# Other warm-ups for TensorE, weights rounded in halves, and EPS added on GpSimd: a conditional MLP with LayerNorm on one core

## The chip, the cores and the metric

The kernel runs on one core of a Trainium2 chip, in one launch. The metric is the device time in microseconds (us) of that core, as the median of the timed runs. The engines are TensorE (PE, its weight loads PEld), VectorE (DVE), ScalarE (ACT), GpSimd (POOL) and SyncE (SP), which issues most DMAs.

## The reference

For each of 16 batches `x[b]` is 512x512. A condition per batch, read at run time, chooses a network; then follow a residual and a LayerNorm over the last axis:

```python
out_nr  = gelu(x @ w1_nr + b1_nr) @ w2_nr + b2_nr          # condition 0
out_tsr = gelu(x @ w1_tsr + b1_tsr) @ w2_tsr + b2_tsr      # condition 1
h = gelu(x @ w1_sr + b1_sr)                                # condition 2, w1_sr is 512x1024
out_sr = gelu(h @ w2_sr + b2_sr) @ w3_sr + b3_sr           # w2_sr is 1024x512
y = x + chosen
return (y - mean(y)) * rsqrt(var(y) + EPS) * gamma + beta
```

All is float32. The conditions of the sixteen batches are 0, 2, 0, 0, 0, 0, 0, 1, 2, 2, 1, 2, 0, 2, 2, 1: seven of kind 0 (`NR`), three of kind 1 (`TSR`), six of kind 2 (`SR`).

## The kernel before

**Precision.** Each fp32 operand is split into a part rounded to fp32r (`hi`) and the rest (`lo`), and each product of 128x128 by 128x512 is three matmuls: hi·hi, hi·lo and lo·hi (`product`, L243). A batch of kind 0 or 1 has 2 x 16 products, 96 matmuls; one of kind 2 has 32 + 32 + 16 products, 240 matmuls.

**Who does what.** SyncE loads the transposed x (`stage`), the rows of x (`y`) and the weights (`w_raw`, two chunks of 128x512 to a pair). For each batch ScalarE makes `x_hi`, the GELU as `g_hi`, and the GELU again unrounded in the PSUM bank; VectorE takes the differences `x_lo` and `g_lo`. TensorE's last layer leaves four tiles (t = 0 to 3, 128 rows each) in banks 4 to 7. GpSimd has added the bias to the rows of x (`add_bias`, L616); VectorE adds these to the bank (`residual`, L482), takes the statistics (`stats`, `moments`), adds EPS to the variances of two tiles at once (`variance`, L499, semaphore `s_var`), and subtracts the mean and multiplies by gamma (`centre`, L494). GpSimd raises variance + EPS to -0.5 (`deviations`, L620), ScalarE multiplies by that (L437), GpSimd adds beta (`shift`, L628), and SyncE stores. Each engine runs its own program in order; semaphores join them. ScalarE frees a bank for the next batch (`s_acc`) when it takes the centred tile. In the last batch the tiles go one by one (`body_end`).

**Weights.** The first w chunks of kind 0 are made by VectorE and ScalarE at the start. Those of the other kinds are split on GpSimd, in pairs (`split_hi` L590, `split_lo` L595), between its other work in the first batches.

**The start.** TensorE first runs warm-ups on a tile of ones: nine matmuls of 128x512 and fourteen of 128x128 in bf16 (L373, L375), whose result is unused. Then it reads the first condition and starts batch 0 (kind 0). The contraction has four chunks c = 0 to 3. For c = 0 and 1 the order is: four matmuls of x_hi and w_hi (which = 0, output columns j = 0 to 3), four with x_lo (which = 1), four with w_lo (which = 2). They wait for `s_first` (x_hi, from ScalarE, L444), `s_first_w` (w_hi, from VectorE, L570), `s_nr` and `s_x01` (the lo parts, L560). VectorE's order there is: cast of w chunk 0, x_lo, w_lo of chunk 0, then the same of chunk 1, then the lo parts of chunks 2 and 3.

Of the kernel before, what the change touches and what calls it, by code (L numbers as in the profile page):

```python
# [5 lines left out]
P = 128  # L6
NBATCH = 16
T = 512
H = 512
HC = H // P  # L10
TT = T // P
EPS = 1e-5
# [25 lines left out]
FINISHED_BY_OTHERS_END = TT - 1  # L38


N_WARM, N_WARM_SHORT = 9, 14


def conditional_mlp(nc, x, x_t, cond, weights, bias_cols, rows, out):
# [3 lines left out]
    with ctx:  # L48
# [3 lines left out]
        def sem(name):  # L52
            return ctx.enter_context(nc.semaphore(name))
# [50 lines left out]
        s_y, s_acc = sem("s_y"), sem("s_acc")  # L104
        s_row = [sem(f"s_x_row{t}") for t in range(TT)]
        s_xb, s_ev, s_bn, s_mv = sem("s_xb"), sem("s_ev"), sem("s_bn"), sem("s_mv")
        s_var = sem("s_var")
        s_own = sem("s_own")
        s_rstd, s_rstd_end = sem("s_rstd"), sem("s_rstd_end")
        s_v, s_v_end = sem("s_v"), sem("s_v_end")  # L110
# [4 lines left out]
        def take(eng, s, n=1):  # L115
            eng.wait_ge(s, n)
            eng.sem_inc(s, -n)  # L117
# [124 lines left out]
        def _(eng):  # L242
# [36 lines left out]
            def part(j, c, which):  # L279

                dst, n, w = bank[j][:, :], bass.ts(j, P), W1[NR] + c
                a, b = (w_lo if which == 2 else w_hi), (x_lo if which == 1 else x_hi)
                return eng.matmul(dst, a[:, w, n], b[:, c, :], start=c == 0 and which == 0, stop=c == HC - 1 and which == 2)

            def step(kind, read_next):
                if kind == NR:
                    take(eng, s_x01, 1)
                    for c in range(2):
                        eng.wait_ge(s_first, c + 1)
                        eng.wait_ge(s_first_w, c + 1)  # L290
                        for which in range(3):
                            if which == 1:
                                if c == 0:
                                    eng.wait_ge(s_nr, 1)
                                else:
                                    take(eng, s_x01, 1)
                                    x_taken(0)
                            if which == 2:
                                eng.wait_ge(s_nr, 2 + c)
                            for j in range(HC):  # L300
                                part(j, c, which)
                        if c == 0:
                            read_next()
                    take(eng, s_x23, 1)
                    for c in (2, 3):
                        if c == 3:
                            take(eng, s_x23, 1)
                            x_taken(1)
                        eng.wait_ge(s_first, 3 + c)
                        if c == 2:  # L310
                            eng.wait_ge(s_nr, 4)
                        for j in range(2):
                            part(j, c, 0)
                            part(j, c, 1)
                        eng.wait_ge(s_nr, 3 + c)
                        for j in range(2):
                            sums = part(j, c, 2)
                            if c == 3:
                                sums.then_inc(s_h, 1)
                    for j in (2, 3):  # L320
                        for c in (2, 3):
                            for which in range(3):
                                sums = part(j, c, which)
                        sums.then_inc(s_h, 1)
                    eng.wait_ge(s_nr, 8)
                    last_layer(W2[kind], ORDER, claim=True)
                    return
# [42 lines left out]
                last_layer(W3[SR], ORDER_SR, claim=False)  # L370

            for _ in range(N_WARM):
                eng.matmul(bank[7][:, :], ones[:, 0:P], ones, start=True, stop=True)  # L373
            for _ in range(N_WARM_SHORT):
                eng.matmul(bank[7][:, 0:P], ones[:, 0:P], ones[:, 0:P], start=True, stop=True)  # L375
            eng.sem_inc(s_acc, 4)
# [87 lines left out]
        def _(eng):  # L464
# [32 lines left out]
            def variance(t, n=1):  # L497
                take(eng, s_mv, n)
                eng.tensor_scalar(var_eps[:, t:t + n], mv[:, t:t + n, 1], EPS, None, ALU.add).then_inc(s_var, n)  # L499
# [15 lines left out]
            def body(kind, read_next):  # L515
                read_next()
                hidden(kind)
                split_x(0, s_x01, 2)
                split_x(1, s_x23, 2)
                eng.wait_ge(s_rows, 16)  # L520
                for t in range(0, TT, 2):
                    residual(kind, t)
                    residual(kind, t + 1)
                    stats(kind, t)
                    stats(kind, t + 1)
                    moments(kind, t)
                    moments(kind, t + 1)
                    variance(t, 2)
                    centre(kind, t)
                    centre(kind, t + 1)  # L530

# [35 lines left out]

            for c in range(2):
                eng.wait_ge(s_w_piece[c], 16)
                eng.tensor_copy(w_hi[:, c, :], w_raw[:, c, :]).then_inc(s_first_w, 1)  # L570
                x_low(c, c + 1, (s_nr, s_x01)[c])
                eng.wait_ge(s_first_w, c + 1)
                w_low(c, 0)
            x_low(2, 3, s_nr)
            x_low(3, 4, s_x23)
# [10 lines left out]
        def _(eng):  # L586
# [29 lines left out]
                        eng.tensor_tensor(y[:, t, :], y[:, t, :], row[:, kind, :], ALU.add).then_inc(s_xb, 1)  # L616

            def deviations(t, n):
                take(eng, s_var, n)
                eng.tensor_tensor(rstd[:, t:t + n], var_eps[:, t:t + n], power[:, t:t + n], ALU.pow).then_inc(s_rstd, n)  # L620

            def deviation_end(t, done=s_rstd):
# [149 lines left out]
```

## Time and profile before the change

| | us |
|---|---|
| median of 3 timed runs | 559.62 (559.47 to 559.8) |
| the profiled execution | 559.41 |
| its span | 557.7 |
| PE busy | 549.6 (99%) |
| DVE busy | 273.9 (49%) |
| POOL busy | 248.3 (45%) |
| ACT busy | 213.5 (38%) |

The span reaches from the first to the last instruction that the profiler saw in one execution. A row of a timeline gives an instruction's start and duration, or of several of one form in a row (x4) the time from the first one's start to the last one's end. The ends of matmuls are modelled and overlap with the next one's start, so the pace is read from the starts. A row of weight loads (PEld) stands for the matmul that follows it.

### The profile page before, as it was taken

Reading aid. Unit: us, or ns where it says so; the run is one execution under the profiler, and the core shown is the slowest. Engines: PE = TensorE matmul, PEld = TensorE weight load, DVE = VectorE, ACT = ScalarE, POOL = GpSimd, SP = SyncE. Lnnn points to the kernel's source line nnn. Section 1 sums busy time; section 2 is a strip of 40 time slices with the busy share of each in tenths; the row PEclk is TensorE's granted clock in tenths of the full one; section 3 lists DMA queues with packets and bytes.
Section 4 is the critical chain, followed back from the end, with each engine's and each line's share of the span. In section 5 each row is a group of like instructions: output and inputs, shape, how many; then the busy total and the mean of one; then the engine's idle time right before and its main releaser. Section 6 shows DMA issues by size and latency. Waiting matters only on the chain. (4 is left out here: it accounts for less than half of the span.)

```text
span 557.7 us, 8222 instructions
## 1 busy us (share of the span) xinstructions
PE 549.6 (99%) x2423; PEld 453.4 (81%) x2424; DVE 273.9 (49%) x448; ACT 213.5 (38%) x328; POOL 248.3 (45%) x196
## 2 busy tenths in 40 slices
PE   9999999999999999999999999999999999999994
PEld 6888888888888888888888888888888888888883
DVE  5660176775856956114710569112765105601657
ACT  5451336145244354214421452424255124513351
POOL 0979898765674575300430046600174300430056
PEclk9999999999999999999999999999999999999998
DMA  8876405245344444200320044400244100410032
GB/s 313 339 237 190 152 7 196 100 151 188 109 155 145 156 150 141 84 0 0 138 87 0 1 158 142 150 0 0 75 150 159 66 0 29 154 43 0 0 135 91
DMA packets 26370, 61.28 MB, mean 110 GB/s; under 512 B 3058, under 2 KB 3314, under 8 KB 26226
## 3 DMA queue, kind: packets, MB, share of 16 engines
q1 hardware_dynamic: 26208, 60.97, 31.9%
q8 instruction: 6, 0.10, 0.1%
q10 hardware_dynamic: 146, 0.13, 0.1%
q14 instruction: 10, 0.08, 0.1%
HBM read 44.31 MB, written 16.78 MB: 110 GB/s over the span
## 5 line engine op out<-in xcount | busy, mean ns | idle before, releaser
L467 DVE TENSOR_TENSOR g_lo<-bank,g_hi 128x512 fp32r<-128x512 f32 x112 | 77.5, 692 | 251.0 <-DVEq L117 250.9
L415 ACT ACTIVATE g_hi<-bank,bcol 128x512 fp32r<-128x512 f32 x112 | 77.9, 695 | 165.9 <-ACTq L117 164.7
L620 POOL TENSOR_TENSOR rstd<-var_eps,power 128x2 f32<-128x2 f32 x30 | 21.0, 699 | 239.7 <-POOLq L117 239.7
L616 POOL TENSOR_TENSOR y<-y,row 128x512 f32<-128x512 f32 x64 | 95.7, 1514 | 49.1 <-POOLq L117 48.9
L437 ACT ACTIVATE y<-y,rstd 128x512 f32<-128x512 f32 x63 | 42.3, 717 | 166.3 <-ACTq L117 166.3
L244 PE MATMUL bank<-w_hi,g_hi 128*128 128x512 f32 x256 | 99.6, 389 | 0.0
L245 PE MATMUL bank<-w_lo,g_hi 128*128 128x512 f32 x256 | 99.6, 389 | 0.0
L246 PE MATMUL bank<-w_hi,g_lo 128*128 128x512 f32 x256 | 99.6, 389 | 0.0
L244 PE MATMUL bank<-x_hi,w_hi 128*128 128x512 f32 x240 | 93.4, 389 | 0.0
L245 PE MATMUL bank<-x_lo,w_hi 128*128 128x512 f32 x240 | 93.4, 389 | 0.0
L246 PE MATMUL bank<-x_hi,w_lo 128*128 128x512 f32 x240 | 93.4, 389 | 0.0
L628 POOL TENSOR_TENSOR y<-y,row 128x512 f32<-128x512 f32 x63 | 79.5, 1296 | 0.0
L244 PE MATMUL bank<-g_hi,w_hi 128*128 128x512 f32 x192 | 74.7, 389 | 0.0
L245 PE MATMUL bank<-g_lo,w_hi 128*128 128x512 f32 x192 | 74.7, 389 | 0.0
L246 PE MATMUL bank<-g_hi,w_lo 128*128 128x512 f32 x192 | 74.7, 389 | 0.0
L416 ACT ACTIVATE bank<-bank,bcol 128x512 f32<-128x512 f32 x112 | 74.3, 664 | 0.0
L244 PEld LDWEIGHTS bank<-w_hi,g_hi 128*128 128x128 f32 x256 | 48.1, 188 | 10.0
L245 PEld LDWEIGHTS bank<-w_lo,g_hi 128*128 128x128 f32 x256 | 48.1, 188 | 10.0
L246 PEld LDWEIGHTS bank<-w_hi,g_lo 128*128 128x128 f32 x256 | 48.1, 188 | 9.9
L472 DVE TENSOR_TENSOR x_lo<-stage,x_hi 128x1024 fp32r<-128x1024 f32 x30 | 51.6, 1757 | 4.3 <-DVEq L117 4.3
L245 PEld LDWEIGHTS bank<-x_lo,w_hi 128*128 128x128 f32 x240 | 45.1, 188 | 9.3
L246 PEld LDWEIGHTS bank<-x_hi,w_lo 128*128 128x128 f32 x240 | 45.1, 188 | 9.3
(42 smaller groups left out, 580.2 us busy)
## 6 DMA issues: line engine op xcount, KB each, us to landing
y<-x SPq DMA_DIRECT2D x64, 256.0 KB, 3.6
out<-y SPq DMA_DIRECT2D x63, 256.0 KB, 2.5
stage<-x_t SPq DMA_DIRECT2D x31, 512.0 KB, 3.3
w_raw<-weights SPq DMA_DIRECT2D x17, 512.0 KB, 5.1
row<-rows SPq DMA_DIRECT2D x1, 1280.0 KB, 11.0
stage<-x_t SPq DMA_DIRECT2D x2, 256.0 KB, 3.2
w_raw<-weights SPq DMA_DIRECT2D x2, 256.0 KB, 4.0
out<-y SPq DMA_DIRECT2D x1, 128.0 KB, 1.9
```

Of the source, the lines that this page charges most:

```text
L244: eng.matmul(dst, a_hi, b_hi, start=first, stop=False)
L245: eng.matmul(dst, a_hi, b_lo, start=False, stop=False)
L246: return eng.matmul(dst, a_lo, b_hi, start=False, stop=final)
L415: eng.activation(g_hi[:, slot, :], psum, ACT.Gelu, bias=b)
L416: eng.activation(psum, psum, ACT.Gelu, bias=b).then_inc(s_g, 1)
L437: eng.activation(y[:, t, :], y[:, t, :], ACT.Copy, scale=rstd[:, t:t + 1]).then_inc(s_n, 1)
L467: eng.tensor_tensor(g_lo[:, slot, :], psum, g_hi32[:, slot, :], ALU.subtract).then_inc(s_gs, 1)
L472: eng.tensor_tensor(x_lo[:, c, :], stage[:, f, :, :], x_hi32[:, c, :], ALU.subtract).then_inc(done, n)
L616: eng.tensor_tensor(y[:, t, :], y[:, t, :], row[:, kind, :], ALU.add).then_inc(s_xb, 1)
L620: eng.tensor_tensor(rstd[:, t:t + n], var_eps[:, t:t + n], power[:, t:t + n], ALU.pow).then_inc(s_rstd, n)
L628: eng.tensor_tensor(y[:, t, :], y[:, t, :], row[:, R_BETA, :], ALU.add).then_inc(s_fin, 1)
```

## The change

Three edits.

1. TensorE's warm-ups are fifteen of 128x307 and seven of 128x128, where there were nine of 128x512 and fourteen of 128x128.
2. VectorE casts each of the first two w chunks in two halves of 256 columns. TensorE waits for a half before output columns j = 0 and j = 2 of the first pass, rather than for the whole chunk ahead of it.
3. For tiles 0 and 1 of the first fifteen batches, GpSimd adds EPS in `deviations`, ahead of its pow; VectorE hands it the moments (`s_moments`) and goes on to `centre`. For tiles 2 and 3 and for the last batch nothing changes.

```diff
-N_WARM, N_WARM_SHORT = 9, 14
+N_WARM, N_WARM_SHORT, WARM = 15, 7, 307
...
-                        eng.wait_ge(s_first_w, c + 1)
...
                             for j in range(HC):
+                                if which == 0 and j % 2 == 0:
+                                    eng.wait_ge(s_first_w, 2 * c + j // 2 + 1)
                                 part(j, c, which)
...
             for _ in range(N_WARM):
-                eng.matmul(bank[7][:, :], ones[:, 0:P], ones, start=True, stop=True)
+                eng.matmul(bank[7][:, 0:WARM], ones[:, 0:P], ones[:, 0:WARM], start=True, stop=True)
...
-                    variance(t, 2)
+                    if t == 0:
+                        take(eng, s_mv, 2)
+                        eng.sem_inc(s_moments, 2)
+                    else:
+                        variance(t, 2)
                     centre(kind, t)
...
                 eng.wait_ge(s_w_piece[c], 16)
-                eng.tensor_copy(w_hi[:, c, :], w_raw[:, c, :]).then_inc(s_first_w, 1)
+                for half in (slice(0, H // 2), slice(H // 2, H)):
+                    eng.tensor_copy(w_hi[:, c, half], w_raw[:, c, half]).then_inc(s_first_w, 1)
                 x_low(c, c + 1, (s_nr, s_x01)[c])
-                eng.wait_ge(s_first_w, c + 1)
+                eng.wait_ge(s_first_w, 2 * c + 2)
                 w_low(c, 0)
...
             def deviations(t, n):
-                take(eng, s_var, n)
+
+                if t == 0:
+                    take(eng, s_moments, n)
+                    eng.tensor_scalar(var_eps[:, t:t + n], mv[:, t:t + n, 1], EPS, None, ALU.add).then_inc(s_eps, n)
+                    take(eng, s_eps, n)
+                else:
+                    take(eng, s_var, n)
                 eng.tensor_tensor(rstd[:, t:t + n], var_eps[:, t:t + n], power[:, t:t + n], ALU.pow).then_inc(s_rstd, n)
```

TensorE at the start of the program, before (const-bfloat16-1.0 is the tile of ones):

```order
2 L373 MATMUL bank<-const-bfloat16-1.0 128x512 x9
3 L375 MATMUL bank<-const-bfloat16-1.0 128x128 x14
4 L136 TENSOR_LOAD cond_sb
5 L406 UNCONDITIONAL_BRANCH
6 L393 COMPARE_AND_BRANCH
```

and now:

```order
2 L374 MATMUL bank<-const-bfloat16-1.0 128x307 x15
3 L376 MATMUL bank<-const-bfloat16-1.0 128x128 x7
4 L136 TENSOR_LOAD cond_sb
5 L407 UNCONDITIONAL_BRANCH
6 L394 COMPARE_AND_BRANCH
```

The widths and counts of the warm-ups change and nothing else moves; the real matmuls behind them (L283) are in the same order.

VectorE at the end of batch 0, before (bn and mv are the statistics and moments):

```order
20 L487 BN_STATS bn<-bank 128x6 x2
21 L491 BN_AGGR mv<-bn 128x2 x2
22 L499 TENSOR_SCALAR var_eps<-mv 128x2
23 L494 SCALAR_TENSOR_TENSOR y<-bank,mv,row 128x512 x2
24 L482 TENSOR_TENSOR bank<-bank,y 128x512 x2
```

and now:

```order
20 L488 BN_STATS bn<-bank 128x6 x2
21 L492 BN_AGGR mv<-bn 128x2 x2
22 L495 SCALAR_TENSOR_TENSOR y<-bank,mv,row 128x512 x2
23 L483 TENSOR_TENSOR bank<-bank,y 128x512 x2
24 L488 BN_STATS bn<-bank 128x6 x2
```

The TENSOR_SCALAR on the variances of tiles 0 and 1 is gone, and the centring follows the moments.

GpSimd in the same place, before:

```order
18 L616 TENSOR_TENSOR y<-y,row 128x512 x2
19 L620 TENSOR_TENSOR rstd<-var_eps,power 128x2
20 L590 TENSOR_SCALAR w_hi<-w_raw 128x1024
21 L620 TENSOR_TENSOR rstd<-var_eps,power 128x2
22 L595 TENSOR_TENSOR w_lo<-w_raw,w_hi 128x1024
```

and now:

```order
18 L622 TENSOR_TENSOR y<-y,row 128x512 x2
19 L628 TENSOR_SCALAR var_eps<-mv 128x2
20 L632 TENSOR_TENSOR rstd<-var_eps,power 128x2
21 L596 TENSOR_SCALAR w_hi<-w_raw 128x1024
22 L632 TENSOR_TENSOR rstd<-var_eps,power 128x2
```

The addition stands between the last bias add and the first pow, ahead of the split of the weights.

## Rows read from the trace of the kernel before

**Rows 1.** The page: busy time, share of the span and instructions of each engine.

```profile
PE 549.6 (99%) x2423; PEld 453.4 (81%) x2424; DVE 273.9 (49%) x448; ACT 213.5 (38%) x328; POOL 248.3 (45%) x196
```

**Rows 2.** Stretches, TensorE alone: from:to, length, busy (instructions), granted clock, DMA share, GB/s.

```profile
6.00:550.00 544.00, 544.00 (x2402) 1.00 0.32 109
2.00:4.00 2.00, 2.00 (x6) 1.00 0.94 311
553.00:554.00 1.00, 0.00 (x0) 0.50 0.63 240
```

**Rows 3.** Timeline of the start, TensorE: start, duration, engine, line, what.

```profile
0.82 4.00 PE L373 MATMUL bank<-const-bfloat16-1.0 128*128 128x512 bf16 x9 [0.82 <-PEq L766]
2.05 0.15 PEld L373 LDWEIGHTS bank<-const-bfloat16-1.0 128*128 128x128 bf16 x1 [0.28 <-issue]
4.61 1.43 PEld L375 LDWEIGHTS bank<-const-bfloat16-1.0 128*128 128x128 bf16 x13 [0.28 <-issue]
6.07 0.55 PE L283 MATMUL bank<-x_hi,w_hi 128*128 128x512 f32 x1
6.46 0.63 PE L283 MATMUL bank<-x_hi,w_hi 128*128 128x512 f32 x2
6.69 0.62 PE L283 MATMUL bank<-x_hi,w_hi 128*128 128x512 f32 x2
7.15 1.07 PE L283 MATMUL bank<-x_lo,w_hi 128*128 128x512 f32 x4
8.96 1.07 PE L283 MATMUL bank<-x_hi,w_hi 128*128 128x512 f32 x4
11.68 0.39 PE L283 MATMUL bank<-x_hi,w_hi 128*128 128x512 f32 x1
```

**Rows 4.** Timeline of the end: TensorE's last matmul.

```profile
550.01 0.39 PE L246 MATMUL bank<-w_hi,g_lo 128*128 128x512 f32 x1
```

**Rows 5.** Timeline of the start, VectorE and ScalarE: where the first operands come from.

```profile
3.40 0.62 ACT L444 CAST x_hi<-stage 128x512 fp32r<-128x512 f32 x1 [0.57 <-DMA stage<-x_t]
4.43 0.43 DVE L570 CAST w_hi<-w_raw 128x512 fp32r<-128x512 f32 x1 [3.53 <-DMA w_raw<-weights]
7.05 0.43 DVE L570 CAST w_hi<-w_raw 128x512 fp32r<-128x512 f32 x1 [0.99 <-DMA w_raw<-weights]
7.40 0.68 DVE L560 TENSOR_TENSOR x_lo<-stage,x_hi 128x512 fp32r<-128x512 f32 x1
```

**Rows 6.** Timeline from batch 0 to batch 1, VectorE and GpSimd.

```profile
26.23 2.53 POOL L616 TENSOR_TENSOR y<-y,row 128x512 f32<-128x512 f32 x2
27.64 1.14 DVE L499 TENSOR_SCALAR var_eps<-mv 128x2 f32<-128x2 f32 x1
28.70 1.40 DVE L494 SCALAR_TENSOR_TENSOR y<-bank,mv,row 128x512 f32<-128x512 f32 x2
28.97 0.72 POOL L620 TENSOR_TENSOR rstd<-var_eps,power 128x2 f32<-128x2 f32 x1 [0.21 <-POOLq L117]
30.02 1.28 DVE L482 TENSOR_TENSOR bank<-bank,y 128x512 f32<-128x512 f32 x2
33.33 0.70 POOL L620 TENSOR_TENSOR rstd<-var_eps,power 128x2 f32<-128x2 f32 x1 [2.60 <-POOLq L117]
```

**Rows 7.** One line (durations ns min/median/max), and GpSimd's smallest operation.

```profile
L499 DVE TENSOR_SCALAR var_eps<-mv x34: 136/169/1142, 27.6 to 553.1; 128x2 f32<-128x2 f32 x30, 128x1 f32<-128x1 f32 x4
...
0.78 0.10 POOL L645 MEMSET power<- 128x4 f32 x1 [0.29 <-POOLq L766]
```

**Rows 8.** Timeline of batch 1: first g_lo and its matmul, fourth split and its matmul.

```profile
37.65 1.47 DVE L467 TENSOR_TENSOR g_lo<-bank,g_hi 128x512 fp32r<-128x512 f32 x2 [3.20 <-DVEq L117]
38.88 0.39 PE L244 MATMUL bank<-g_hi,w_hi 128*128 128x512 f32 x1
41.20 2.40 POOL L595 TENSOR_TENSOR w_lo<-w_raw,w_hi 128x1024 fp32r<-128x1024 f32 x1 [0.18 <-POOLq L117]
44.32 0.39 PE L244 MATMUL bank<-x_hi,w_hi 128*128 128x512 f32 x1
```

More of the change, by code:

```diff
@@ L106, in conditional_mlp @@
         s_xb, s_ev, s_bn, s_mv = sem("s_xb"), sem("s_ev"), sem("s_bn"), sem("s_mv")
-        s_var = sem("s_var")
+        s_moments, s_eps, s_var = sem("s_moments"), sem("s_eps"), sem("s_var")
         s_own = sem("s_own")
```

## The prediction

> **What bounds the kernel now.** I read the page's busy shares first: TensorE is busy 549.6 of 557.7 us, the next engine 49% of the span [rows 1]. That alone would not tell a queue full of waits from a full engine, so next comes a table of stretches: from 6 to 550 us TensorE is busy in every microsecond [rows 2]. Real matmuls start at 6.07 and the last one starts at 550.01 [rows 3, 4]; there are 2400 of them (seven batches of kind 0 and three of kind 1 with 96, six of kind 2 with 240), so the mean pitch is 543.94/2399 = 0.2267 us, the same as between two early matmuls (6.69 - 6.46). There is no stall to remove between 6.07 and 550. The time is therefore: start of the first real matmul, plus 2400 pitches, plus what the clock costs at the start, plus a tail of 557.7 - 550.0 = 7.7 us, plus 1.7 us outside of the span (the profiled execution took 559.41). The median of the timed runs is 559.62, 0.21 above it; I work out a difference and take it from the median.
>
> Then the start, row by row. A warm-up of 512 columns takes 0.427 us ((4.61 - 2.05)/6), one of 128 columns 0.107 ((1.43 - 0.15)/12) [rows 3]: 1200 columns in a microsecond, so the engine is at its lower level of 1.2 GHz. The granted clock printed for these stretches is 1.00 [rows 2], so that column has no record there and the pitch has to be read instead; the 0.50 behind the last matmul shows that the lower level does exist in it. Among the real matmuls the first starts at 6.07, the second at 6.46, the third at 6.69 [rows 3]: 0.39, then 0.23. So the rise to 2.4 GHz falls within the first real matmul, which lost 0.39 - 0.227 = 0.16 us; at half speed that is 0.33 us of cold time, and the rise lies at 6.07 + 0.33 = 6.40 at the latest.
>
> **Part 1: the warm-ups.** Removed: 9 x 0.427 + 14 x 0.107 = 5.34 us. Added: a warm-up of 307 columns at the same 1.2 columns per ns takes 307/512 x 0.427 = 0.256, so 15 x 0.256 + 7 x 0.107 = 4.59 us. (No row has this width; the bounds are the two forms seen, and by both the cost goes with the columns, so neither end differs by more than 0.02 us for the group.) The array is free at 6.07 - 0.75 = 5.32 us. Are the operands there? The first x chunk is rounded at 3.40 + 0.62 = 4.02, the first w chunk at 4.43 + 0.43 = 4.86 [rows 5]: yes, 0.46 us ahead. So the real work starts 0.75 us earlier, and what it gains depends on when the clock rises. If this stays at 6.40 of the program, the stretch from 5.32 to 6.40 is worked at half speed: 0.54 us of full work is done by 6.40, against 0.17 before. Gain 0.37 us, half of the 0.75. If the rise comes before 5.32, the gain is all 0.75. I take 0.37, because the rise was seen at one place only, and keep both ends.
>
> [...] The rows put the rise 5.6 us after the first warm-up, in one execution. [...]
>
> **Part 2: the halves.** VectorE's cast of 128x512 takes 0.43 us [rows 5]. Half of it takes at least 0.21, and at most 0.43 (no saving at all); the smallest VectorE operations shown, of one and two columns, take 0.14 to 0.17 [rows 7], so I take 0.17 + 0.13 = 0.30. Each chunk then costs VectorE 0.60 in place of 0.43, +0.17 (bounds 0 and +0.43); TensorE's waits for a half at 4.73 in place of 4.86, which the warm-ups hide. What is late next? With the real work at 5.32 and the clock rising at 6.40, each later group of four starts 0.37 before its row of now [rows 3]: chunk 0 asks for x_lo at 7.15 - 0.37 = 6.78, chunk 1 for w_hi at 8.96 - 0.37 = 8.59 and for its x_lo four matmuls (0.91) later, at 9.50, and chunk 2 starts at 11.31. Ready is w_hi of chunk 1 at 7.05 + 0.43 = 7.48 and its x_lo at 7.40 + 0.68 = 8.08 [rows 5], each plus 0.17 where the halves stand ahead of it; x_lo of chunk 0 follows the cast of chunk 0 directly (4.86 + 0.17 and some 0.7 for an operation like it, 5.7). The closest is w_hi of chunk 1, 7.48 + 0.17 = 7.65 against 8.59: 0.94 us ahead. With a start that gains all of the 0.75, and halves at +0.43, 0.3 us are left (7.91 against 8.21). Cost 0.
>
> **Part 3: EPS on GpSimd.** Fifteen batches, one operation each. On VectorE the operation costs 0.17 us as a rule, but 1.14 in the first batch, from 27.64 to 28.78, where GpSimd's add of the bias ends at 28.76 [rows 6, 7]. Without it the centring at 28.70 starts about 1.1 earlier, and with it the residual at 30.02, whose operands are there (the bias of the last tile at 28.76). GpSimd instead does: add (between 0.10, its smallest operation, a memset [rows 7], and 0.72, the pow of the same shape; I take 0.2), 0.2 of a wait for its own semaphore (0.18 to 0.21 in its rows), then the pow. The first two tiles' rstd comes 0.4 later in the first batch, and ScalarE scales them by so much later. Behind the new wait on GpSimd stand split_hi, the second pow (33.33, after 2.60 us of idle time) and all the splits of weights for kind 2; the idle time absorbs 0.4 to 0.9 and the second pow itself is called 1.1 earlier by VectorE. In later batches GpSimd has no splits between its pows (busy 45% of the span in all [rows 1]) and the same slack, and VectorE saves 0.2. None of this is on TensorE's path: value 0 by itself.
>
> It matters as cover. The second batch is of kind 2, and its first consumer of g_lo starts at 38.88, while g_lo of that chunk, anchored at the end of batch one's vector work, is done at 37.65 + 0.69 = 38.34 [rows 8]: 0.54 us of slack. Part 1 eats 0.37 to 0.75 of it; part 3 gives about 1.1 back. Likewise the fourth split of w1 is done at 43.60 and its matmul starts at 44.32 [rows 8]: 0.72, which would go to nothing at worst, and grows by the 1.1 as well.
>
> **Sum.** -0.37 (start and clock) + 0 (halves) + 0 (EPS) = -0.37 us: 559.41 becomes 559.04 by the profiled execution, and 559.62 becomes 559.25 by the median.
>
> **Rivals.**
> A, the clock rises before the real work, at least in most runs: gain 0.75, 558.87. For it: a rise that falls within 0.3 us of the end of the warm-ups looks like chance. Against it: four executions lie within 0.39 us. [...]
> B, the gain is capped in batch two: part 3 doesn't bring the 1.1 us (VectorE's next instruction waits for the same thing that held the 1.14 us one), and the first g_lo of kind 2 binds at 38.34. Then no more than 0.54 is gained, 559.08 where A holds; and if the splits come 0.9 late on top (0.72 + 0.18 on GpSimd), the matmul at 44.32 slips by 0.18 and the time is 559.8. Against it: the centring now runs beside GpSimd's pow and split_hi at 1.40/2 = 0.70 apiece [rows 6], so it isn't held by GpSimd's work as such.
> C, slower: the clock rises later. If the narrower warm-ups don't count for the clock like those of 512 columns, and the rise comes as far behind the first real matmul as it now comes behind the first warm-up (6.40 - 0.82 = 5.6 us), it comes at 10.9; the 4.5 us from 6.40 on at half speed cost 2.25, net of the gain +1.9: 561.5. It costs more than is gained as soon as the rise slips by over 0.75 us. Against it: the array is fed without a gap in both forms, with the same columns in a microsecond.
> D, nothing: the start is held by the first operands rather than the warm-ups. Only if the transfers land 0.46 us later than in this execution; then the gain shrinks to nothing, 559.6.
>
> **Chances.** Forecast (gain about 0.37, 559.25) 0.43; A 0.29; B 0.07; D 0.10; C 0.04; the rest, 0.07, for something unseen. The likeliest case's own range is 558.9 to 559.6. The range of 8 in 10 takes in A, B and D and the 0.3 us by which runs differ: 558.5 to 560.1. About 0.2%, 1.1 us, is what a measurement of this kernel can tell from no change; faster by more needs a gain over 1.12, which no case has (0.05, out of the unseen); slower by more is C, with 0.01 of the unseen (0.05); within it 0.90.
>
> **What would show it.** First real matmul at about 5.3; the first two pitches at 0.43, the third in between and 0.23 from about 6.4 on (forecast), or none at 0.43 (A), or ten or more (C). Casts of 0.3 us. No VectorE operation of over 1 us near 27.6, and the residual of 30.02 near 28.9. The first g_lo of batch two at about 36.6. TensorE busy in every microsecond from the first real matmul on, and its last matmul 0.37 (or 0.75) earlier, with an unchanged tail of 7.7. The prediction is wrong if a gap appears in TensorE's row, if the warm-ups of 307 columns don't take 0.256, or if the tail changes.

## The result, and the profile after: 0.9 us slower, with a gap behind batch 0

The changed kernel takes 560.55 us (median of 14 runs, 560.32 to 561.37), the kernel before on the same chip 559.67 (559.43 to 560.43): a ratio of 1.0016, with an interval of 1.0008 to 1.0023. It is slower by 0.88 us, which the interval tells from no change; the prediction said 559.25, with 558.5 to 560.1 as the range of 8 in 10, so the time lies outside of it. The profiled execution took 560.88, its span 558.9. (One run of e6 below took 616.34 us at a granted clock of 0.85; its ratio leaves it out.)

One view shows most of it: the stretch in which TensorE was busy in every microsecond before [rows 2]. From:to, length, busy (matmuls), granted clock, DMA share, GB/s, in the kernel after:

```profile
6.00:550.00 544.00, 542.75 (x2394) 1.00 0.32 109
...
27.00:28.00 1.00, 0.84 (x4) 1.00 0.33 66
28.00:29.00 1.00, 0.00 (x0) 1.00 0.86 270
29.00:30.00 1.00, 0.91 (x4) 1.00 1.03 279
```

1.25 us are missing, all between 27 and 30. What TensorE waited for (us in total, times, longest):

```profile
PE bank L244 <- PEq L117: 1.3, 1, 1.3
PE bank L374 <- PEq L778: 0.8, 1, 0.8
PE bank L283 <- DVE w_hi L576: 0.5, 1, 0.5
```

The second row was there before. The third is rival D's wait, the first was foreseen nowhere: its releaser is PEq, TensorE's own sequencer, and no other engine's semaphore is named. TensorE's timeline after (answers to [rows 3, 4]):

```profile
0.82 4.01 PE L374 MATMUL bank<-const-bfloat16-1.0 128*128 128x307 bf16 x15 [0.82 <-PEq L778]
4.62 0.68 PE L376 MATMUL bank<-const-bfloat16-1.0 128*128 128x128 bf16 x7
5.82 1.17 PE L283 MATMUL bank<-x_hi,w_hi 128*128 128x512 f32 x4 [0.51 <-DVE w_hi L576]
...
27.45 0.39 PE L246 MATMUL bank<-w_hi,g_lo 128*128 128x512 f32 x1
29.09 0.47 PE L244 MATMUL bank<-x_hi,w_hi 128*128 128x512 f32 x1 [1.25 <-PEq L117]
...
551.23 0.39 PE L246 MATMUL bank<-w_hi,g_lo 128*128 128x512 f32 x1
```

and the same seam in the kernel before, where the two batches join at one pitch (28.00 - 27.77 = 0.23):

```profile
27.77 0.39 PE L246 MATMUL bank<-w_hi,g_lo 128*128 128x512 f32 x1
28.00 0.39 PE L244 MATMUL bank<-x_hi,w_hi 128*128 128x512 f32 x1
```

So batch 0 ended 0.32 earlier (27.45 against 27.77), then 1.64 - 0.23 = 1.41 was lost at the seam and some 0.1 in the pitches behind it; the last matmul starts 1.22 later than before (551.23 against 550.01 in [rows 4]). The tail is as it was (558.9 - 551.23 = 7.7).

Between the batches TensorE's program jumps. The code of kind 0 ends with `eng.br("tensor_kinds_end")`, a branch over the code of the other kinds (line 390 before, 391 after). Its row (count, then ns min/median/max, first and last start), before:

```profile
L390 PEldq COMPARE_BRANCH  x16: 184/194/449, 23.9 to 546.2; - x16
```

and after:

```profile
L391 PEldq COMPARE_BRANCH  x16: 184/194/3586, 23.6 to 547.4; - x16
```

The first jump takes 3.59 us in place of 0.45. The queue runs 3.8 us ahead of the array (the jump starts at 23.9 before and 23.6 after, the last matmul of batch 0 at 27.77 and 27.45), which hid the jump of 0.45 and not this one: it ends at 23.6 + 3.59 = 27.2, and the first matmul of batch 1 comes 1.9 us later. No row names what it waits for; what fits is in the DMA queues (packets, MB, share). The first block of instructions (16 KB; the page counts six, q8) comes at 21.2 to 21.5 in the kernel before:

```profile
q1 hardware_dynamic: 62, 0.11, 100.6%
q8 instruction: 1, 0.02, 21.9%
```

and at 24.5 to 24.8 after, behind a stretch (20 to 24.5, second fence) that moved data alone:

```profile
q1 hardware_dynamic: 21, 0.05, 39.2%
q8 instruction: 1, 0.02, 21.4%
```

```profile
q1 hardware_dynamic: 718, 1.81, 105.1%
```

The packet starts at 21.34 before and 24.62 after, and the jump ends 2.6 us behind that (27.2 - 24.62). That the jump waits for this packet is read from the times: in all nine profiles of this document with one late block it ends 2.58 or 2.59 us behind the packet's start, whether this lies 0.07 ahead of the jump (e1) or 1.60 behind it (e18).

The same sum holds for what follows. In the nine profiles of this document with one late block, batch 1 starts 4.40 to 4.48 us behind the start of the fetch (here 29.09 - 24.62 = 4.47), although batch 0 ended anywhere from 26.80 to 28.54 in them. Nor does the late fetch follow the start: it comes at 24.31 to 24.94 for starts from 5.11 to 6.89. With a late fetch the start of the real work is thus out of the sum: whatever batch 0 gains is waited away at the seam.

**The median's 0.88 in two parts.** The time outside of the span is 1.97 us on average in the ten programs (with the experiments) in which `s_first_w` has reached four at the end, and 1.75 in the others, where it has reached two: +0.21. The rest, 0.67, lies in the span, whose median goes from 557.9 to 558.6. The two profiled executions differ by more (557.7 and 558.9), because the one before is 0.2 shorter than its median and the one after 0.3 longer.

### The profile page after: what moved, and what is told of

It reads as the page before. It is cut to its first block and busy times, and to the rows that moved or that the text cites. A ratio compares the mean times of both kernels' runs of the same rounds, so it can differ in the third digit from the quotient of the medians.

```text
span 558.9 us, 8252 instructions
## 1 busy us (share of the span) xinstructions
PE 549.0 (98%) x2422; PEld 453.0 (81%) x2423; DVE 271.2 (49%) x435; ACT 213.6 (38%) x328; POOL 252.0 (45%) x211
## 5 line engine op out<-in xcount | busy, mean ns | idle before, releaser
L628 POOL TENSOR_SCALAR var_eps<-mv 128x2 f32<-128x2 f32 x15 | 3.3, 218 | 186.4 <-POOLq L117 186.3
L244 PEld LDWEIGHTS bank<-x_hi,w_hi 128*128 128x128 f32 x240 | 45.0, 188 | 10.9 <-issue 1.6
```

What stands on the lines that cost most here:

```text
L244: eng.matmul(dst, a_hi, b_hi, start=first, stop=False)
```

## The experiments

Times are medians with range and count; the ratio is to the kernel before on the same chip. Jumps (when the first one starts, and how long it takes), fetches, seams and the start of batch 1 are of the one profiled execution of each.

| | median (range, runs) | ratio, interval | first fetch | first jump at | it takes, us | seam | batch 1 at |
|---|---|---|---|---|---|---|---|
| e1 | 560.27 (559.18-560.65, 11) | 1.0005 [0.9996, 1.0014] | 24.64 | 24.71 | 2.51 | 0.57 | 29.12 |
| e2 | 560.01 (559.58-560.79, 11) | 1.0006 [0.9997, 1.0015] | 24.74 | 23.62 | 3.71 | 1.77 | 29.22 |
| e3 | 560.65 (560.34-561.45, 11) | 1.0017 [1.0008, 1.0026] | 24.70 | 23.54 | 3.75 | 1.80 | 29.17 |
| e4 | 560.89 (560.70-561.11, 11) | 1.0018 [1.0009, 1.0027] | 24.89 | 23.76 | 3.71 | 1.77 | 29.36 |
| e5 | 559.36 (558.98-560.31, 11) | 0.9996 [0.9987, 1.0005] | 22.22 | 23.53 | 1.27 | none | 27.59 |
| e6 | 560.03 (559.28-616.34, 11) | 1.0003 [0.9994, 1.0012] | 22.02 | 24.52 | 0.45 | none | 28.58 |
| e7 | 559.12 (558.68-559.83, 11) | 0.9993 [0.9983, 1.0002] | 21.01 | 23.60 | 0.45 | none | 27.66 |
| e8 | 559.54 (one) | | 21.53 | 24.05 | 0.45 | none | 28.11 |
| e9 | 559.78 (559.42-560.26, 11) | 1.0001 [0.9992, 1.0010] | 21.66 | 23.71 | 0.57 | none | 27.77 |
| e10 | 559.83 (559.27-561.17, 11) | 1.0005 [0.9996, 1.0014] | 20.64 | 23.23 | 0.44 | none | 27.29 |
| e11 | 560.22 (558.86-560.70, 11) | 1.0001 [0.9992, 1.0011] | 24.31 | 23.48 | 3.41 | 1.47 | 28.78 |
| e12 | 558.96 (558.75-559.63, 11) | 0.9990 [0.9981, 0.9999] | 22.19 | 23.74 | 1.34 | none | 27.80 |
| e13 | 560.81 (560.36-561.16, 10) | 1.0015 [1.0005, 1.0024] | 24.94 | 23.86 | 3.67 | 1.72 | 29.42 |
| e14 | 559.35 (558.91-562.4, 10) | 0.9997 [0.9985, 1.0009] | 21.98 | 23.58 | 0.85 | none | 27.63 |
| e15 | 560.02 (559.48-563.14, 10) | 1.0011 [0.9998, 1.0025] | 21.94 | 23.95 | 0.61 | none | 28.01 |
| e16 | 560.77 (560.35-561.71, 10) | 1.0021 [1.0011, 1.0031] | 24.56 | 23.50 | 3.65 | 1.71 | 29.04 |
| e17 | 562.11 (561.9-563.73, 6) | 1.0047 [1.0034, 1.0059] | 24.74, 24.89 | 23.67 | 5.32 | 3.09 | 30.59 |
| e18 | 560.47 (560.30-560.88, 10) | 1.0013 [1.0003, 1.0022] | 24.57 | 22.97 | 4.18 | 2.17 | 28.97 |

The seam is the time from the last matmul's start in batch 0 to the first one's in batch 1; 0.23 is "none".

**e1, the kernel before with one short warm-up fewer.** `N_WARM_SHORT = 13`.

> The kernel before with 13 warm-ups of 128 columns in place of 14, and nothing else. Theory L (place in the program): the changed kernel loses 1.4 us where TensorE's queue jumps from the end of batch 0's code to the loop's end, because its code for TensorE is one warm-up (a weight load and a matmul) shorter, and the block of instructions it jumps to is no longer fetched ahead. Then this kernel has the same gap between batch 0 and batch 1 (a jump of 3.6 us in place of 0.45, TensorE idle 1.4 us), and is slower by about 1.3 us, since the missing warm-up gives 0.05 to 0.11 back. Theory T (time): the jump is late in the changed kernel because the start is earlier or the transfers differ. Then there is no gap here, and the time is that of before less 0.05 to 0.11 us.

The fetch came at 24.64, 0.07 before the jump, which took 2.51. So a late fetch needs none of the three edits: the kernel before with one warm-up fewer has one too. The times tell less than the profile: 559.2 to 560.7, where the kernel before took 558.8 to 561.0 on this chip.

**e2, Part 1 alone.**

```diff
-N_WARM, N_WARM_SHORT = 9, 14
+N_WARM, N_WARM_SHORT, WARM = 15, 7, 307
```

> The kernel before with the new warm-ups alone (fifteen of 307 columns, seven of 128). Theory L: TensorE's code is shorter by one warm-up, as in the changed kernel: gap of 1.4 us behind batch 0, slower than before by 0.7 to 1.1 us (1.4 lost, 0.37 to 0.75 gained at the start). A rival, P (parts): the gap comes from the halves' waits on TensorE or from the operation moved to GpSimd; then there is no gap here and the time is 0.3 to 0.7 us below before.

The warm-ups ended early (start at 5.13), and the seam cost 1.5. The same gap, without halves and without EPS. The profiled execution is the slowest of the eleven (560.79), though; the median, 560.01, is 0.10 over the kernel before, so the gap can't be in all of them.

**e3, the changed kernel with eight short warm-ups.** `N_WARM_SHORT = 8`.

> The changed kernel with eight warm-ups of 128 columns in place of seven, so that TensorE's code is as long as before. Theory L: no gap behind batch 0 (the jump takes 0.45 us), and the time is 0.3 to 0.65 us below before: the start gains 0.64 of warm-ups, half or all of it as the clock rises. Theories T and P: the gap of 1.4 us stays, and the time is that of the changed kernel plus 0.05 to 0.1.

0.1 us more of warm-ups moves nothing: a fetch at 24.70, 1.80 at the seam.

**e4, Part 2 alone.**

```diff
-                        eng.wait_ge(s_first_w, c + 1)
+                                if which == 0 and j % 2 == 0:
+                                    eng.wait_ge(s_first_w, 2 * c + j // 2 + 1)
...
-                eng.tensor_copy(w_hi[:, c, :], w_raw[:, c, :]).then_inc(s_first_w, 1)
+                for half in (slice(0, H // 2), slice(H // 2, H)):
+                    eng.tensor_copy(w_hi[:, c, half], w_raw[:, c, half]).then_inc(s_first_w, 1)
...
```

> The kernel before with the casts of the first two weight chunks in halves alone, and TensorE's waits for a half. Theory L: TensorE's code is as long as before, no gap; the time is that of before within 0.1 us, since the warm-ups hide the casts. Theory P (the halves' waits make the gap): a gap of 1.4 us and 1.4 us slower.

Slower by 0.98: all of the change's loss, and with the old warm-ups and no Part 3 hardly more of it than the whole change's 0.88. An early start saves almost nothing where the fetch is late. Every one of the 11 times is above 560.6, which fits a late fetch in all of them, where in e1 and e2 the times spread over 559.2 to 560.8.

**e5 and e6, holding transfers back.** SyncE waits before the weight pairs of the other kinds (`POOL_ALL`) until GpSimd has added the bias to the first tiles of batch 0; in the changed kernel (e5) and in the one before (e6).

```diff
+            eng.wait_ge(s_go, 1)
             landed = POOL_FIRST + POOL_ALL
...
+                    eng.sem_inc(s_go, 1)
```

> The changed kernel, with SyncE holding back the weight loads of the later kinds (twelve of 512 KB) until GpSimd has issued the bias of tiles 0 and 1 of batch 0, at about 21 to 25 us. In the five programs with a late jump the first instruction block of TensorE is fetched at 24.6 to 24.9 us, when the first run of transfers ends, whether the jump comes before or behind it; in the kernel before it was fetched at 21.3. Theory Q (queue): the fetch stands behind the transfers that are under way. Two pairs, 1.05 MB at about 400 GB/s, less stand ahead of it, so it starts about 2.6 us earlier, at 22.0 to 22.5; the jump is then done at 24.6 to 25, there is no gap between batch 0 and 1, and the time is 1.3 to 1.5 us below the changed kernel. Theory J (the jump itself asks for the block): the fetch stays 1.0 us behind the jump, at 24.6, and the gap of 1.4 us stays.

> The same holding back in the kernel before. Theory Q: the fetch starts by 22.5 in every execution; the runs that were slow (to 561) move to the fast end, and the median falls by 0.3 to 0.6 us to 559.3 to 559.5; beside the changed kernel with the same holding back (e5) this is slower by 0.37 to 0.75, what the earlier start is worth. Theory J: no change against before in time or spread.

The five programs that e5's expectation starts from are the changed kernel and e1 to e4: first fetch at 24.62 to 24.89, jump at 23.5 to 23.8 in four and at 24.71, behind the fetch, in e1. Their transfers moved 396 to 402 GB/s from 20 to 24.5 (DMA share 1.04 to 1.05), and the share fell to 0.41 to 0.84 in the half microsecond from 24.5 on. The kernel before has the same fall (1.03 from 23 to 24, 0.21 from 24.5 to 25) and its fetch at 21.34, 3 us ahead of it. With the hold (e5) the share falls from 0.97 (21 to 22) to 0.36 (22 to 23), and the fetch starts at 22.22.

e5's jump:

```profile
L392 PEldq COMPARE_BRANCH  x16: 184/194/1266, 23.5 to 545.8; - x16
```

and its queues from 22.1 to 22.4:

```profile
q8 instruction: 1, 0.02, 21.2%
q1 hardware_dynamic: 11, 0.01, 11.9%
```

TensorE's and VectorE's programs are those of the changed kernel, and the seam is gone: 559.36, 1.19 under the changed kernel's 560.55 on another chip (each against the kernel before of its chip: -0.39 and +0.88). So the gap, the late fetch and the transfers hang together. In the kernel before, whose fetch was early, the hold gains nothing (e6).

**e7, Part 3 alone** (of the diff, GpSimd's side).

```diff
-                take(eng, s_var, n)
+                if t == 0:
+                    take(eng, s_moments, n)
+                    eng.tensor_scalar(var_eps[:, t:t + n], mv[:, t:t + n, 1], EPS, None, ALU.add).then_inc(s_eps, n)
+                    take(eng, s_eps, n)
...
```

> The kernel before with the addition of EPS for tiles 0 and 1 on GpSimd alone. TensorE's code and start are those of before. Expected by my account of this part (off the path): within 0.2 us of before where the fetch comes at the same time. If the fetch is late in this program too (start near 24.6), 1 us slower, with a gap of 1.1 to 1.4 us behind batch 0 and nowhere else; in either case the first g_lo of batch 1 is done over 1 us ahead of its matmul.

559.12, 0.63 under before, an interval that just touches no change. In its trace the clock had risen at 3.9, so that even the old warm-ups ended at 5.3:

```profile
0.82 3.61 PE L373 MATMUL bank<-const-bfloat16-1.0 128*128 128x512 bf16 x9 [0.82 <-PEq L776]
...
5.35 1.17 PE L283 MATMUL bank<-x_hi,w_hi 128*128 128x512 f32 x4
```

An execution like this, without Part 3, would meet the first `g_lo` of batch 1, as e9 and e10 show next.

**e8, the kernel before again.**

> The kernel before once more, unchanged, for a second look at its fetch. Theory V (varies by execution): the fetch starts at another time than 21.3, anywhere up to 24.9, with a gap behind batch 0 where it is later than about 22. Theory F (fixed by the program): it starts at 21.3 again, and there is no gap.

Start 6.07 and fetch at 21.53, as in the first profile; the first matmul's pitch is 0.47 where it was 0.39, so the clock rose a little later.

**e9 and e10, the halves taken apart.** e9 has the four casts, but TensorE waits for whole chunks; e10 the waits for halves, but one cast a chunk, which raises the semaphore by 2 (shown against e4).

```diff
-                for half in (slice(0, H // 2), slice(H // 2, H)):
-                    eng.tensor_copy(w_hi[:, c, half], w_raw[:, c, half]).then_inc(s_first_w, 1)
+                eng.tensor_copy(w_hi[:, c, :], w_raw[:, c, :]).then_inc(s_first_w, 2)
```

> The kernel before with VectorE's two casts in halves, while TensorE waits for both halves where it waited for the whole. TensorE's code is that of before, instruction for instruction. In e4 (casts and waits) all runs were slow, 560.7 to 561.1, with a late fetch; e1 and e2 (another number of warm-ups) had some fast runs. Theory W (TensorE's own code decides when the fetch gets through: its waits and length): here nothing is late; 559.5 to 559.9, and no gap behind batch 0. Theory D (VectorE's code or timing decides): 560.7 to 561.1 and the gap, as e4.

> The kernel before with TensorE's waits placed as for halves, while VectorE casts the whole chunk at once and raises the semaphore by two. It isn't a wait that costs by itself: the operands are ready as before. Theory W: 560.7 to 561.1, first fetch at 24.6 to 24.9, a gap of 1.4 to 1.8 us behind batch 0, as e4. Theory D: time of before (559.5 to 559.9), no gap.

Neither profile has the late fetch, so neither casts nor waits bring it by themselves as they do together. Both have the +0.21 outside of the span. And both lack Part 3, and show what it covers. e10's TensorE, where batch 1 turns from x to g:

```profile
37.95 0.39 PE L246 MATMUL bank<-x_hi,w_lo 128*128 128x512 f32 x1
38.52 0.47 PE L244 MATMUL bank<-g_hi,w_hi 128*128 128x512 f32 x1 [0.18 <-issue]
```

A pitch of 0.57 in place of 0.23. e10's VectorE:

```profile
28.07 1.14 DVE L500 TENSOR_SCALAR var_eps<-mv 128x2 f32<-128x2 f32 x1
...
37.72 0.69 DVE L468 TENSOR_TENSOR g_lo<-bank,g_hi 128x512 fp32r<-128x512 f32 x1 [2.84 <-DVEq L117]
```

`g_lo` is done at 38.41 and its matmul starts at 38.52. Rival B's limit is real, in the form of a kernel that starts early without Part 3; e9 has it as well (0.49 before 38.91, `g_lo` done at 38.81). The 0.54 us of slack that the prediction read were those of one execution: e8 and e15, with the same start of 6.07, have 0.35 and 0.28.

**e11 and e12, Parts 1 and 3 without the halves** (the changed kernel with e4's diff reversed), e12 with e5's hold besides.

> The new warm-ups and EPS on GpSimd, without the halves. By theory W with the length alone (as e2, whose runs went from 559.6 to 560.8): 559.3 to 560.5, mixed, fast where the fetch is early. By theory D: always early, since VectorE's casts are whole: 558.7 to 559.1, that is e7 less the 0 to 0.4 us by which the warm-ups end earlier.

> As e11, with the later weight loads held back as in e5. Theory Q (the fetch stands behind transfers under way): its first fetch starts by 22.3 in every run, no gap; 558.6 to 559.2, the fastest version, 0.3 to 0.5 under e5 and 0.7 to 1 under before. If holding back has a price of its own (the weights come late for GpSimd's splits), the time is that of e11 or above it.

e11's times fall into two groups, 558.86 to 559.32 (five) and 560.22 to 560.70 (six), 1.3 apart, and its profiled run, of the upper one, has the seam. By the sum of the first section a fetch at 24.31 fixes all that follows it (last matmul at 550.88, 560.28 in all), so the lower group must have fetched earlier: the same program does both. None of the lower group was profiled. With the hold the times are 558.75 to 559.63: a median of 558.96, the best version, 0.71 under before and 1.26 under e11 on the same chip. Its windows and its jump:

```profile
6.00:550.00 544.00, 544.00 (x2400) 1.00 0.32 109
```

```profile
L391 PEldq COMPARE_BRANCH  x16: 184/194/1336, 23.7 to 546.0; - x16
```

No gap from 6 to 550, and a start at 5.33.

**e13, e14, e15, more and fewer transfers in flight.** e13 (changed kernel) and e15 (before) let four weight pairs be in flight in place of two; e14 is e5 with the rows of tiles 2 and 3 held back too.

```diff
-                eng.wait_ge(s_loaded[landed[landed.index(item) - 2]], 16)
+                if landed.index(item) >= 4:
+                    eng.wait_ge(s_loaded[landed[landed.index(item) - 4]], 16)
```

> The changed kernel with four weight loads of 512 KB in flight where there were two, so that the first run of transfers ends about 2.6 us later (1.05 MB more at 400 GB/s), near 27.2 us. Dose up. Theory Q (the fetch of the instruction block waits for the transfers under way): first fetch at about 27.2, the jump done 2.59 us behind it, batch 1 starts at about 31.7, the gap is 4 us and the time 563.1. If the fetch is tied to the jump instead (1.0 us behind it): 24.6 again, a gap of 1.4, 560.5.

> The changed kernel with the later weights held back as in e5, and the rows of tiles 2 and 3 of batch 0 as well, so that the first run of transfers ends 1.3 us earlier than in e5 (0.52 MB less), at about 20.9. Dose down. Theory Q: first fetch at about 20.9 (or, if asked for only later, at that moment, which would show when it is asked for), jump in 0.45 us, no gap; 559.3 as e5 or 0.1 less, unless the late rows hold GpSimd and through it the first g_lo of batch 1 (over 1 us of cover).

> The kernel before with four weight loads in flight. In its two profiles the first fetch came at 21.3 and 21.5, while transfers were under way. Theory Q without exception: it is only luck that it gets through, so in part of the runs it waits until about 27.2 and they take 562 to 563; the spread grows to some 3.5 us. Theory E (in this program the fetch has a way past the transfers): first fetch at 21.3 again, all runs at 559.4 to 560.2 as before.

In e13 transfers run on to 28.5 (DMA share 1.04 from 24 to 26, 1.01 from 26 to 28, 0.98 from 28 to 28.5; 389 to 408 GB/s up to 28, near the 400 of the expectation), yet the fetch comes at 24.94, amid them:

```profile
q1 hardware_dynamic: 33, 0.11, 96.0%
q8 instruction: 1, 0.02, 21.5%
```

So the block doesn't wait for the data queues to drain: that theory falls. e15's fetch stays early (21.94) under the same load in the profiled execution (559.51), but three of its ten times are 560.88 to 563.14, over all 31 of the kernel before (at most 560.25), and none of these was profiled: late fetches in part of the runs aren't ruled out there. In e14 transfers had ended at about 21 (DMA share 0.78 from 20 to 20.5, 0.35 from 20.5 to 21, 0.08 from 21 to 22) and the fetch came at 21.98, only 0.24 earlier than in e5 and not as early as without any hold (20.64 to 21.66 in e7 to e10): less load doesn't bring it at once either.

**e16, the changed kernel again.**

> The changed kernel once more, unchanged. Its first 14 runs took 560.32 to 561.37 without exception. If the late fetch is the rule of this program: again all above 560.3, first fetch between 24.5 and 24.9. If each launch draws anew: some runs at 559.0 to 559.4.

The seam repeats (1.71, jump 3.65), here with a start at 5.34 and not 5.82: the late weights of the first profile are not its cause. With the first series these are 24 timed runs, none under 560.3.

**e17 and e18, the hint.** The jump carries a branch hint from the beginning of the kind's code (in the trace BRANCH_PREFETCH_HINT in TensorE's queue, first at 4.4 before and 3.3 after). e17 is the kernel before without it; e18 the changed kernel with kind 0's hint placed ahead of the last layer only, where the queue passes it at 12.1 (the expectation says 14.5).

```diff
-                        ahead = eng.mark_branch_hint_location()
                         step(kind, read_next)
-                        eng.br("tensor_kinds_end").branch_hint(ahead)
+                        eng.br("tensor_kinds_end")
```

> The kernel before without the hints that name the target of the jump at the end of each kind's code ahead of it. [...] Theory H (in the changed kernel the block asked for ahead doesn't come, and the jump itself has to fetch it): in the slow programs the fetch starts 1.0 to 1.16 us behind the jump in six of eight profiles, with few or many transfers under way. So here: first fetch at about 25.0 (jump at 23.95 and 1.05), the jump 3.6 us long, a gap of 1.1 to 1.7 us behind batch 0; time 560.7 to 561, like the changed kernel, in all runs. If the hint has no part in it: time and fetch of before (21.3, 559.7).

> The changed kernel with the hint of batch kind 0 not at the start of its code but ahead of its last layer (TensorE's queue is there at about 14.5 us in place of 3.3). Theory H2 (the hint comes too early, before the wait for the late operands, and is lost): with the later hint the block is fetched ahead, before 22 us, no gap; 559.1 to 559.4. If where the hint stands is no matter: 560.6, first fetch 1.0 to 1.1 us behind the jump.

e17's jump:

```profile
L389 PEldq COMPARE_BRANCH  x16: 169/169/5322, 23.7 to 548.9; - x16
```

and its queues from 24.6 to 25.0, two blocks at once:

```profile
q8 instruction: 2, 0.03, 56.6%
q1 hardware_dynamic: 29, 0.06, 39.9%
```

Without the hint the fetch starts 1.07 behind the jump, and the kernel is 2.07 slower. In the changed kernel it starts 24.62 - 23.62 = 1.0 behind the jump, and in e2, e3, e4, e13 and e16 1.06 to 1.16: as late as without the hint, though with one block rather than two. But in all six the jump comes at 23.5 to 23.9, so that they can't tell "one us behind the jump" from "at 24.6 to 24.9". e1 and e18, whose jumps come at 24.71 and 22.97, can: their fetches start at 24.64, before the jump, and at 24.57, 1.6 behind it. So in e1 it wasn't the jump that set off the fetch; over the nine profiles the fetch stays within 24.31 to 24.94 while its distance from the jump moves by 1.7 us. For the others it isn't settled. A later hint (e18) doesn't mend it.

## Why the prediction was wrong, point by point

**The step that failed** is in "What bounds the kernel now" and "What would show it": TensorE is busy in every microsecond from the first real matmul on, so the time is start plus pitches plus tail, and an earlier start shifts all that follows. Two things were left out of the sum, TensorE's instruction fetch and its queue's lead of 3.8 us over the array. With the fetch at 24.62, batch 1 could not start before 29.09, and 1.41 us were lost at the seam, more than the whole gain; the 0.21 outside of the span came on top. The prediction named the sign of it ("wrong if a gap appears in TensorE's row") but gave only 0.07 to something unseen, split over both sides. The trace of before held the signs: six fetches in its list of queues, a jump with a maximum of 449 ns against a median of 194, and DMA busy for 8 tenths of the two slices up to 28 us. Rows 1 to 8 hold none of them.

**Part 1, the warm-ups.** 0.256 us for 307 columns was right: fifteen of them lie between 0.82 and 4.62 in the timeline after, 3.80/15 = 0.253. The start was to be 5.32: it was 5.33 in e5 and e12, 5.34 in e16, and 5.82 in the first profile, where the first cast came late:

```profile
5.37 0.49 DVE L576 CAST w_hi<-w_raw 128x256 fp32r<-128x256 f32 x2 [4.47 <-DMA w_raw<-weights]
```

That is rival D, in part of the runs. What the early start gives, no run splits off. e12 is 0.71 under before, but e7, with the old warm-ups and Part 3, is 0.63 under it, and the difference is inside the noise. In the profiles batch 0's last matmul starts at 26.80 to 27.69 with the new warm-ups (ten programs, median 27.39) and at 27.07 to 28.54 with the old ones (ten, median 27.68): some 0.3 earlier, nearer to my 0.37 than to rival A's 0.75, in spreads that are wider than the difference. The moment of the rise did vary: read from the pitches it lies at 3.5 (e2), 3.9 (e7), 4.9 (after), 6.0 (e16) and 6.65 (e12). The changed kernel alone had it at 4.9 and 6.0, and the spread over all programs is 3 us; what sets the moment, no run shows. Nor does a row give the clock in GHz: the prediction's 1.2 is an estimate from the 1200 columns in a microsecond of the warm-ups [rows 3], its 2.4 and the half speed are estimates from that and the granted clock of 0.50 [rows 2]. Measured are paces: 307 columns in 0.256 us before the rise and 0.135 behind it (e2, weight loads at 3.70 and 3.97, two warm-ups apart), 128 in 0.107 and 0.058 (e7, twelve from 4.28 to 4.98), 512 of a real matmul in 0.43 (e12, its second) and 0.227. The pace before the rise is thus 0.53 to 0.55 of that behind it, which is 2200 to 2280 columns in a microsecond. My anchor at 6.40 rested on one execution, and on a pitch of 0.227 for a first matmul at the high clock. The later profiles show 0.31 there (e4, e9, e10, e17) and 0.57 with the clock still low (0.572 to 0.575 in e5, e11, e12, e13, e14 and e16), not my 0.43, so that I estimate the rise in the kernel before, with half speed again, at 6.07 + 2 x (0.39 - 0.31) = 6.23. Rival C (a rise at 10.9) did not happen anywhere.

**Part 2, the halves.** The size was right: 0.30 expected, and

```profile
L576 DVE CAST w_hi<-w_raw x4: 285/288/295, 5.4 to 7.2; 128x256 fp32r<-128x256 f32 x4
```

The cost of 0 was wrong: e4 alone is +0.98, of which 0.21 lies outside of the span (in e9 and e10 too, so it goes with a semaphore that ends at four) and 0.77 in the span, in a program whose profile lost 1.54 at the seam. Neither was in the sum, since both lie outside of what the halves touch by the program's data flow.

**Part 3, EPS on GpSimd.** Right in its prices and in what it covers. GpSimd's addition takes 0.22 (0.2 expected), with 0.18 of its own wait:

```profile
28.69 0.22 POOL L628 TENSOR_SCALAR var_eps<-mv 128x2 f32<-128x2 f32 x1
29.09 0.72 POOL L632 TENSOR_TENSOR rstd<-var_eps,power 128x2 f32<-128x2 f32 x1 [0.18 <-POOLq L117]
```

and VectorE's chain (answers to [rows 6, 8]) is 1.1 earlier at the centring and the residual, 1.4 at the first `g_lo`, though batch 1 itself began 1.09 later. Some of it is the execution, in which GpSimd's adds of the bias ended at 28.61 against 28.76. Where GpSimd was equally far (e7 and e9, 29.64 and 29.58), Part 3 is worth 0.9: the centring at 28.62 against 29.52, the first `g_lo` done at 37.90 against 38.81. The first pow is 0.12 later, where I had said 0.4. The rows after:

```profile
27.60 1.41 DVE L495 SCALAR_TENSOR_TENSOR y<-bank,mv,row 128x512 f32<-128x512 f32 x2 [0.25 <-DVEq L117]
28.93 1.29 DVE L483 TENSOR_TENSOR bank<-bank,y 128x512 f32<-128x512 f32 x2
36.21 0.69 DVE L468 TENSOR_TENSOR g_lo<-bank,g_hi 128x512 fp32r<-128x512 f32 x1 [2.84 <-DVEq L117]
```

That cover is worth something, where the sum had 0: e9 and e10 without it lose 0.26 and 0.34 at 38.5 to 38.9, and e7 with it gains 0.63 (an interval of 0.9983 to 1.0002, so it isn't clear of noise).

**What is shown:** the place and size of the gap; that it is the jump's wait, which ends some 2.6 us after a fetch that starts at 24.3 or later, so that batch 1 starts 4.4 to 4.5 behind the fetch whatever the start gained; that the same TensorE code with the fetch at 22.2 has no gap (e5 against the changed kernel); that the hint matters by 2 us (e17). **What stays open:** why the block comes at 20.6 to 22.2 in some executions and at 24.3 to 24.9 in others. The length of the code isn't it (e3), nor casts or waits alone (e9, e10), nor a drained queue (e13), nor, in e1 at least, the jump, nor the hint's place (e18), nor late weights (e16). It comes late in every profile with both casts and waits in halves and no hold, in the profiles of e1, e2 and e11, and by the times in part of their runs only. The moment of the request against the transfers around 20 to 22 us would fit e5 and e11, but this was only argued. The cause of the 0.21 outside of the span is open as well.

## What to carry to other kernels

Busy in every microsecond means that operands are in time, not that an earlier start is passed on: look at the sequencer's own rows, the jumps and the instruction queue, at the first crossing into new code, and at how far the queue runs ahead of the array (3.8 us here). A jump with an outlier in its maximum (449 ns against a median of 194), beside DMA that is nearly full (a share of 1.03 to 1.07 from 20 to 24 us in the kernel before), is where edits elsewhere cost 1.41 us here; a hold of transfers that aren't yet needed, until the fetch had started, removed it here. Where such a wait binds, measure how far behind the fetch the next work starts: a gain ahead of it is worth nothing. And where one program's times fall into two groups, take the two apart, and profile one of each, before crediting an edit with their difference.

## What the runs showed of the hardware

- The first jump took 0.44 or 0.45 us where the fetch had started 2.5 to 2.6 us ahead of it (before, e6, e7, e8, e10), 0.57 to 1.34 for 1.3 to 2.1 us ahead (e5, e9, e12, e14, e15), 2.51 for 0.07 ahead (e1), 3.4 to 4.2 where the fetch started 0.8 to 1.6 us behind the jump, and 5.3 where two blocks came at once (e17). Where one block was late, the jump ended 2.6 us behind the start of its fetch and the array went on 1.9 later (29.09 - 27.2).
- Over all profiled executions the clock's rise came between 3.5 (e2) and 6.65 us (e12), as read from the pitches, and the first weights' cast started between 4.33 (e11) and 6.31 (e1).
- VectorE's addition of EPS to 128x2 took 1.14 us beside GpSimd's add of the bias [rows 6], 0.17 in the median [rows 7]; the longest one after the change is 171 ns. In all ten profiles without Part 3 it took 1.10 to 1.15 and ended within 0.03 us of GpSimd's add.
- The time outside of the span was 1.97 us in the ten programs with `s_first_w` at four in the end, and 1.75 in the others, which do the same work.
